# A new written-out order for the loop of a two-block vision kernel: fewer changes of TensorE's tiling

## Time and profile before

| | |
|---|---|
| runs of the kernel before | 370.17, 370.65, 375.33 us; median 370.65 |
| profiled execution, first to last instruction (its span) | 370.4 us |
| what lies around the span | 0.25 us, taken as the median less the span (the profile gives the profiled execution no other time than its span) |
| busy: PE, DVE, ACT, POOL | 331.5, 264.2, 235.4, 95.8 us |
| granted TensorE clock, mean of the span | 0.966 of 2.4 GHz |
| last matmul | starts 364.74, 1.08 us long |

### The profile page before, as it was taken

How to read it: one execution, slowest core, us unless ns; L and a number is a source line. 1 busy time by engine, 2 the same in 40 slices (tenths; PEclk the granted TensorE clock), 3 DMA queues, 4 the chain that set the end, 5 groups by cost and what they waited for, 6 DMA issues and landing times.

```text
span 370.4 us, 5249 instructions
## 1 busy us (share of the span) xinstructions
PE 331.5 (90%) x1709; PEld 177.8 (48%) x1709; DVE 264.2 (71%) x532; ACT 235.4 (64%) x448; POOL 95.8 (26%) x83
## 2 busy tenths in 40 slices
PE   8967999999967676789999899999999899898994
PEld 6556787878943133443434344344344344243230
DVE  3466978789543447779778969969958959947862
ACT  3533767778635453567678659769759766656653
POOL 6224374664410112412005103103105103102000
PEclk9989999999988969699999999999999999999999
DMA  5961000000000000039192193193193095075573
GB/s 152 146 202 32 3 1 2 0 3 2 2 0 2 0 1 0 0 112 354 43 386 86 33 357 117 33 356 115 35 374 96 4 327 173 0 259 215 191 308 65
DMA packets 27724, 42.48 MB, mean 115 GB/s; under 512 B 15857, under 2 KB 17649, under 8 KB 27697
## 3 DMA queue, kind: packets, MB, share of 16 engines
q1 hardware_dynamic: 27696, 42.14, 36.1%
HBM read 39.25 MB, written 2.88 MB: 114 GB/s over the span
## 4 chain that ended last, share of the span: by engine, by line
PE 32%; DVE 27%; DMA 12%; issue 10%; POOL 7%; SPq 6%; ACT 4%; POOLq 1%; ACTq 0%; DVEq 0%
DMA GB<-spread 9%; POOL rstdA L545 5%; PE ps L800 5%; PE ps L911 4%; PE ps L722 4%; DVE HB L1311 3%; PE ps L678 3%; DVE varA L1202 2%; SPq L486 2%; DVE XC L1311 2%; PE ps L709 2%; PE ps L690 2%; DMA spread<-GT 1%; DVE XN L1207 1%; DVE XN L1209 1%
## 5 line engine op out<-in xcount | busy, mean ns | idle before, releaser
L800 PE MATMUL ps<-ET,W1B 64*128 64x512 f32 x256 | 69.0, 641 | 1.4 <-ACT HB L1521 1.4
L1311 DVE TENSOR_TENSOR HB<-HB,GB 128x1024 f32<-128x1024 f32 x44 | 53.1, 1221 | 17.6 <-DMA GB<-spread 13.7
L1521 ACT ACTIVATE HB<-ps,B1B 128x1024 f32<-128x1024 f32 x44 | 48.1, 1114 | 15.5 <-PE ps L800 15.1
L545 POOL TENSOR_TENSOR rstdA<-varA,pow_half 128x8 f32<-128x8 f32 x16 | 30.4, 1897 | 74.1 <-DVE varA L1202 74.1
L911 PE MATMUL ps<-HB,W2B 128*64 128x512 f32 x176 | 44.8, 608 | 0.9 <-DVE HB L1311 0.9
L545 POOL TENSOR_TENSOR rstdB<-varB,pow_half 128x8 f32<-128x8 f32 x8 | 14.9, 1865 | 112.4 <-DVE varB L1244 112.4
L800 PEld LDWEIGHTS ps<-ET,W1B 64*128 64x128 f32 x256 | 21.3, 189 | 29.0 <-issue 17.7
L545 POOL TENSOR_TENSOR rstd<-var,pow_half 128x4 f32<-128x4 f32 (+1 forms) x24 | 29.1, 1219 | 22.9 <-DVE var L1015 13.9
L1311 DVE TENSOR_TENSOR XC<-XC,GB 128x1024 f32<-128x1024 f32 x20 | 24.1, 1220 | 7.1 <-DMA GB<-spread 6.7
L849 PE MATMUL ps<-VP,WC 128*128 128x512 f32 x96 | 27.3, 428 | 0.7 <-ACT VP L1484 0.7
L560 POOL TENSOR_TENSOR QS<-QS,rqsum 128x512 f32<-128x512 f32 x16 | 17.0, 1060 | 30.2 <-DVE rqsum L1076 30.2
(11 more groups left out here) (225 smaller groups left out, 627.7 us busy)
## 6 DMA issues: line engine op xcount, KB each, us to landing
GB<-spread SPq DMA_DIRECT2D x64, 512.0 KB, 8.0
out<-W1stage SPq DMA_DIRECT2D x8, 256.0 KB, 2.9
XC<-in_x SPq DMA_DIRECT2D x6, 256.0 KB, 5.7
G3R<-spread_r SPq DMA_DIRECT2D x48, 16.0 KB
T<-in_x SPq DMA_DIRECT2D x1, 512.0 KB, 3.7
W1A<-in_w1a SPq DMA_DIRECT2D x1, 512.0 KB
W1B<-in_w1b SPq DMA_DIRECT2D x1, 512.0 KB
spread_r<-KV SPq DMA_DIRECT2D x8, 64.0 KB, 9.9
```

The lines of the kernel that those rows point to most:

```text
L545: pool.tensor_tensor(out_, var, pow_half[:, 0:n], ALU.pow).then_inc(s[rstd_sem], 1)
L800: mm(ps[:, H_BANKS[n % 2][c], :], weights[half(c), :], tokens(half(c)), start=True, stop=True).then_inc(s["h"], 1)
L1311: tt(HG[b][e], HG[b][e], GB[:, e, :], ALU.mult).then_inc(s["f_hg"], 1)
L1521: av(HG[b][e], HID[n % 2], ACT.Gelu, bias=B1B[:, e:e + 1]).then_inc(s["gelu"], 1)
```

## The change

`FIRST`, `PLAN`, `LAST` and the code that expands them go; one list `LOOP` holds the whole order of the loop for each engine, every part with its image. The same parts stand in it, each once, with the same code, waits and buffers. The attention's order is also written out (`ATTENTION`), and is the same order; a part that issued nothing (`set_warm2`, zero matmuls; `order_rows` for pairs above 0) is dropped. The order on POOL is unchanged, and SP's code is not touched. On PE, ACT and DVE the order of the loop differs:

- **PE**: 137 runs instead of 154. Counted by stretches that end with `b_gates_turned:b` for b = 0 to 7, and the rest: before 11, 15, 18, 21, 21, 21, 23, 12, 12; after 11, 14, 18, 21, 17, 20, 17, 8, 11. The runs that go are 5 H, 7 O and 5 F.
- **PE, start**: `f_start:0` behind `b_gates:0`; `a_vT1:1` ahead of `f_hidden0:0 f_hidden1:0`; `b_conv0:1 b_conv1:1` ahead of `f_hidden2:0`.
- **PE, middle**: `b_conv0` and `b_conv1` side by side, and behind them `f_hidden4` beside `a_hidden1`; for image 2 and 3, `f_output5`, `f_hidden2` and `a_hidden0` of the next image stand ahead of or behind `b_gates_turned` in new places; `b_gates_turned:4` comes directly behind `f_hidden1:4`.
- **ACT and DVE** follow: at the start `a_square0:0` ahead of `a_select:1`, `a_z_copy:1` ahead of `a_select:2`, `b_exp:0` ahead of `a_image0:1 a_image1:1`, `f_gelu0:0` behind `b_gates_out:0`; in the middle `b_scale` ahead of `f_gelu4`; at the end several `f_gated:5` behind `a_normalise:7`.

The core of the diff, cut to TensorE's list and to the code:

```diff
-    for b in STEADY:
-        period(b, b % 2, PLAN[name], parts, image_exists)
-    in_order(LAST[name])
+    assert {token.split(":")[0] for token in LOOP[name]} == set(parts)
+    in_order(LOOP[name], parts)
...
     pe, start, before:
-        "a_z_turned:2 f_start:0 b_to_channels:0 b_gates:0 a_vT0:1 f_hidden0:0 f_hidden1:0 a_vT1:1 b_gates_turned:0 f_hidden2:0 "
-        "b_conv0:1 b_conv1:1 b_to_tokens:1 f_hidden3:0 f_hidden4:0 f_hidden5:0 f_output0:0 f_hidden6:0 f_hidden7:0 "
     and after:
+        "a_z_turned:2 b_to_channels:0 b_gates:0 f_start:0 a_vT0:1 a_vT1:1 f_hidden0:0 f_hidden1:0 b_gates_turned:0 "
+        "b_conv0:1 b_conv1:1 f_hidden2:0 b_to_tokens:1 f_hidden3:0 f_hidden4:0 f_hidden5:0 f_output0:0 f_hidden6:0 f_hidden7:0 "
...
     pe, the period before (b+1 is written +1):
-        "f_start f_output2-1 f_hidden0 f_hidden1 f_output3-1 f_output4-1 f_output5-1 b_gates_turned f_hidden2 "
-        "a_hidden0+2 a_vT0+1 f_hidden3 a_vT1+1 f_output6-1 b_conv0+1 f_hidden4 b_conv1+1 a_hidden1+2 b_to_tokens+1 "
-        "f_bias-1 a_output+2 f_output7-1 a_z_turned+2 f_hidden5 f_hidden6 f_output0 f_output1 b_to_channels+1 "
-        "f_hidden7 b_gates+1"
     and images 3 to 4 of the list after:
+        "f_hidden0:3 f_hidden1:3 f_output2:2 f_output3:2 f_output4:2 f_output5:2 f_hidden2:3 a_hidden0:5 "
+        "b_gates_turned:3 a_vT0:4 f_hidden3:3 a_vT1:4 f_output6:2 b_conv0:4 b_conv1:4 f_hidden4:3 a_hidden1:5 "
+        "b_to_tokens:4 a_output:5 f_hidden5:3 a_z_turned:5 f_bias:2 f_output7:2 f_output0:3 f_output1:3 f_hidden6:3 "
+        "b_to_channels:4 f_hidden7:3 b_gates:4 f_start:4 f_output2:3 f_output3:3 f_output4:3 f_hidden0:4 f_hidden1:4 b_gates_turned:4 "
...
     pe, the end of the list after, from a_output:7 on:
+        "a_output:7 f_hidden5:5 a_z_turned:7 f_bias:4 f_output7:4 f_output0:5 f_output1:5 f_hidden6:5 b_to_channels:6 b_gates:6 f_output2:5 "
+        "f_hidden7:5 f_hidden0:6 f_hidden1:6 f_hidden2:6 a_vT0:7 b_gates_turned:6 a_vT1:7 b_conv0:7 b_conv1:7 "
+        "b_to_tokens:7 f_output3:5 f_output4:5 f_output5:5 f_bias:5 f_start:6 f_output6:5 f_output7:5 f_output0:6 "
+        "b_to_channels:7 b_gates:7 f_hidden3:6 f_hidden4:6 f_start:7 f_output1:6 f_output2:6 b_gates_turned:7 "
+        "f_hidden5:6 f_hidden6:6 f_hidden7:6 f_hidden0:7 f_output3:6 f_hidden1:7 f_hidden2:7 f_output4:6 f_output5:6 "
+        "f_bias:6 f_hidden3:7 f_hidden4:7 f_output6:6 f_output7:6 f_output0:7 f_output1:7 f_hidden5:7 f_hidden6:7 "
+        "f_hidden7:7 f_output2:7 f_output3:7 f_output4:7 f_output5:7 f_output6:7 f_bias:7 f_output7:7"
```

More of the change, by code:

```diff
@@ L109 @@
     ).split(),
     act=(
-        "f_gelu5-1 a_select+2 b_channels f_gelu6-1 f_gelu7-1 b_exp a_square1+1 f_gelu0 f_gelu1 b_gates_out f_gelu2 "
-        "a_image0+1 a_image1+1 a_hidden0+2 f_gelu3 f_gelu4 b_scale+1 a_hidden1+2 a_z_copy+2 b_square+1 f_result-1 "
-        "a_square0+2"
[14 rows of a table added]
     ).split(),
 )
-ATTENTION_PLAN = dict(
+LOOP = dict(
     pool=(
-        "rstd2_3-1 rstd1_0+1 rstd1_1+1 qnorm2 rstd2_0 qnorm3 rstd2_1 qnorm0+1 qnorm1+1 rstd2_2"
+        "a_rstd0:0 a_rstd1:0 a_rstd0:1 b_rstd:0 a_rstd1:1 a_rstd0:2 a_rstd1:2 b_rstd:1 b_rstd:2 a_rstd0:3 a_rstd1:3 "
+        "b_rstd:3 a_rstd0:4 a_rstd1:4 b_rstd:4 a_rstd0:5 a_rstd1:5 b_rstd:5 a_rstd0:6 a_rstd1:6 b_rstd:6 a_rstd0:7 "
+        "a_rstd1:7 b_rstd:7"
@@ L120 @@
     ).split(),
     pe=(
[L122 to L146, removed]
[8 rows of a table removed]
[27 rows of a table added]
     ).split(),
@@ L157, with in_order @@
         "a_sum:0 a_ss0:0 a_zn:0 a_residual:0 a_centre:0 a_ss1:0 a_normalise:0 a_sum:1 a_ss0:1 a_zn:1 a_residual:1 "
[2 rows of a table removed]
[2 rows of a table added]
         "b_centre:1 f_gated0:0 b_ss:1 f_gated1:0 f_gated2:0 b_normalise:1 a_normalise:2 f_gated3:0 f_gated4:0 "
[3 rows of a table removed]
[17 rows of a table added]
     ).split(),
     act=(
[6 rows of a table removed]
[18 rows of a table added]
     ).split(),
 )
-LAST = dict(
-    pool=(),
-    pe=(
[7 rows of a table removed]
-    ).split(),
-    vec=(
[5 rows of a table removed]
-    ).split(),
-    act=(
[4 rows of a table removed]
[L197 to L200, removed]
 B_TOP = 14
 LOWEST = -3.0e38
-def parts_of(plan):
-    for token in plan:
-        name = token.rstrip("0123456789").rstrip("+-") if "+" in token or "-" in token else token
-        yield name, int(token[len(name):] or 0)
-def period(b, par, plan, parts, live):
-    for name, ahead in parts_of(plan):
-        if live(name, b, ahead):
-            parts[name](b + ahead, (par + ahead) % 2)
-def periods(name, parts):
-    def image_exists(name, b, ahead):
-        return 0 <= b + ahead < B
-    def in_order(tokens):
-        for token in tokens:
-            part, b = token.split(":")
-            parts[part](int(b), int(b) % 2)
-    assert sorted(parts) == sorted(part for part, _ in parts_of(PLAN[name]))
-    in_order(FIRST[name])
-    for b in STEADY:
-        period(b, b % 2, PLAN[name], parts, image_exists)
-    in_order(LAST[name])
-def pair_periods(name, parts):
-    parts, plan = dict(parts), ATTENTION_PLAN[name]
-    assert sorted(parts) == sorted(name for name, _ in parts_of(plan))
-    for p in range(-MOST_AHEAD, PAIRS + MOST_AHEAD):
-        period(p, p % 2, plan, parts,
-               lambda name, p, ahead: p + ahead == 0 or 0 < p + ahead < PAIRS and not name.startswith("set_"))
+def in_order(tokens, parts):
+    for token in tokens:
+        part, b = token.split(":")
+        parts[part](int(b), int(b) % 2)
+def periods(name, parts):
+    assert {token.split(":")[0] for token in LOOP[name]} == set(parts)
+    in_order(LOOP[name], parts)
+def pair_periods(name, parts):
+    parts = dict(parts)
+    assert {token.split(":")[0] for token in ATTENTION[name]} == set(parts)
+    in_order(ATTENTION[name], parts)
 def largest(vec, steps, p, n, vals, rev, m, eq, rank, q, onehot):
@@ L588, in _ @@
             mm = pe.matmul
-            WARM = (6, 2, 0)
+            WARM = (6, 2)
             def constant_products(bank, count):
@@ L760, in set_second @@
                 mm(ps[0:E, Q_BANK[1], 0:C], B2TA[:, :], ic[0:C, C:P], start=True, stop=True).then_inc(s["set_w2"], 1)
-            pair_periods("pe", [("set_second", set_second), ("set_warm0", set_warm(0)), ("set_warm1", set_warm(1)), ("set_warm2", set_warm(2)), ("set_fold", set_fold), ("set_outputs", set_outputs)] + [(f"{name}{h}", part(h)) for h in range(2) for name, part in (
+            pair_periods("pe", [("set_second", set_second), ("set_warm0", set_warm(0)), ("set_warm1", set_warm(1)), ("set_fold", set_fold), ("set_outputs", set_outputs)] + [(f"{name}{h}", part(h)) for h in range(2) for name, part in (
                                     ("centre", centre), ("xn_to_channels", xn_to_channels),
@@ L999, in part @@
                 def part(p, par):
-                    if p > 0:
-                        return
                     vec.wait_ge(s["ld_x0"], 16)
```

21 lines of the change are left out of this document (16 added, 5 removed), and 124 rows, old and new, of tables (act, pe, pool, vec).

## The result

The changed kernel takes **383.75 us** (median of 4 runs, 382.13 to 383.95) against 372.10 for the kernel before on the same chip (4 runs, 370.17 to 375.33): ratio 1.032, 95% interval 1.028 to 1.036. The forecast was 368.7 with a range from 363.5 to 373: the change was forecast as a gain and is a loss, and the time lies outside the range. The profiled execution has a span of 380.3 us, 9.9 more than before.

The account below looks back on a forecast made before the run. From 164 us on TensorE's own list was taken as the bound; before that, it often waits for a DVE, POOL and ACT chain. Span 370.4 + 0.7 - 1.4 - 0.4 - 0.9 + 0.1 = 368.5, with 0.25 368.7; range 363.5 to 373.

Parts of the forecast that it names:

- Start, forecast +0.7: Start of the loop: `b_to_tokens:1` starts at 164.15 instead of 163.48 us, so the start costs 0.7 us.
- I take 0.25 early: Start: wait before `a_hidden0:2` shrinks to about 1.8 us, clock stays full, `b_gates:0` comes 0.25 us early at 150.95.
- If the clock rises at 157.8 as before: Start: assumes full clock returns at 157.8 us, putting `b_gates_turned:0` at 158.5 instead of 157.84.
- Rival 2: Start: a 0.8 us gap keeps half clock until the convolution is done, +3.95 us, 372.6 in all; chance 0.15.
- a start at half clock twice over: Start: case put outside the range 363.5 to 373, together with an end without idle time under 2 in 10.
- A change of tiling: TensorE's list: each run costs beyond its parts 0.20 us for H, 0.15 for O, 0.20 for F.
- Rival 3: TensorE's list: joined parts of O and F save nothing, 0 and not 2.05 us, giving 370.75; chance 0.08.
- The number of runs: TensorE's list: 17 runs go, eight before `a_output:7` ends (-1.4 us) and nine behind (-1.6 us).
- The waits at `b_gates_turned`: Middle: TensorE's waits there sum to 2.6 us instead of 3.5, -0.9; bounds -3.5 and 0.
- End, forecast +0.1: From 306.58 us to the last matmul: walk gives 59.9, less six roundings 59.3, against 59.2; bounds -1.6 and +1.5.
- Rival 1: Whole kernel: TensorE's list is all that counts, start hidden, no new waits in the end, 365.3 us; chance 0.27.
- The base: Whole kernel: the median time lies 0.25 us above the span, so span 368.5 becomes 368.7.

Follow-up runs that it names:

- joined_conv: Kernel before with `b_conv1` put beside `b_conv0` and `f_hidden4` beside `a_hidden1` for images 3 to 6, 8 runs fewer: 371.06 against 371.02 us, ratio 0.998.
- end_only: Kernel before with the new order only in the end of the loop, nine runs fewer: 376.36 against 372.21 us, ratio 1.011.
- best_a: New start with 21 constant products, old middle with only eight pairs of parts joined, old end: 368.07 us against 372.03 for the kernel before, ratio 0.990.

## Why the prediction was wrong

The forecast for the span was 368.5; it was 380.3. The 11.8 us between are 0.3 ahead of the loop, 5.1 in the start, 2.9 in the middle, 3.5 in the end.

- **Start, forecast +0.7, measured +5.84. The step that failed is "I take 0.25 early"**: that the idle time before `a_hidden0:2` shrinks to about 1.8 us and the clock then stays full. The 1.8 was a slip in the working: with `a_hidden0:1` 2.0 later and `a_hidden0:2` 0.6 later, as the prediction has them, the wait of 3.96 shrinks to 2.6. It measured 2.65, and 2.6 is no longer close to the 1.6 that had left the clock at full. The clock fell all the same, 3.2 us later than before and so under `b_conv0:0`. Relative to the loop's start `b_gates:0` came 2.88 later than forecast. From there `b_gates:0` to `f_hidden0:0` took 4.73, forecast 4.70, at half clock as the forecast had it. Then the second assumption failed, "If the clock rises at 157.8 as before": hidden pair to `b_gates_turned:0` 3.72 instead of 2.85, from there to `b_to_tokens:1` 7.04 instead of 5.65. 2.88 + 0.03 + 0.87 + 1.39 = 5.2, the whole miss. Shown: filled with constant products, the same order takes 45.2.
- **Rival 2 named the mechanism** (gap ahead of the hidden pair, half clock until the convolution is done, the pair at 3.79, which is what it took) but priced one stretch, at 3.95. Two came, and "a start at half clock twice over" was left outside the range. Against its own full-clock time of 45.2 the start lost 8.2; the old start loses 1.8 (47.53 against 45.71), or 0.7 to 0.9 where its first hidden pair is at full clock.
- **A change of tiling, 0.15 to 0.20 per run: right** (`joined_conv`: 0.16 to 0.19). Lone parts cost what they did: a hidden part 1.06 (227.91 to 228.97), an output part 1.00 (219.00 to 220.00). Rival 3, and with it the rule of the Trainium skill (TensorE: Matmul & The Clock Gate, Part 3, The mechanism), would, as the prediction reads it, give `joined_conv` only the 4 runs of H, 0.8; the trace shows 1.3 to 1.6, so joining full-array parts saved time here too.
- **The number of runs: wrong.** The prediction counts `b_gates_turned` as full array, but the trace gives it as 128*64, the outputs' own tiling (it stands so in the earlier trace rows). Counted that way the list goes from 150 to 137 runs, in the middle from 99 to 95 and not from 105 to 97. Four runs at 0.18 and `f_bias:4` are 1.1; TensorE's busy time fell by 0.69 (138.78 to 138.09). Forecast were 1.8. What the last 0.4 are I have not isolated.
- **The waits at `b_gates_turned`, forecast 3.5 to 2.6: wrong in size.** The places were right: none at b = 3, one at b = 4, but that one took 1.70 and not 0.85; and `b_to_channels` waited 0.25 and 0.85, which I had not walked. For b = 5, 0.25 was forecast and 0.15 came. Idle time in the middle went up by 0.90 instead of down by 0.9. But this moves from execution to execution: the old middle took 141.28 to 143.10 in eight, the new one 139.88 to 143.68 in six without half clock. Most of that spread goes with one operation on POOL (last section), which the prediction took as fixed. The forecast gain of 2.7 is not there between the two orders as a whole.
- **End, forecast +0.1.** From `a_output:7` to `a_vT0:7` it took 15.71 (forecast 15.0), to `b_gates_turned:7` 22.29 (20.6; 20.94 with the products), to the last matmul 24.87 (24.3). The walk gave 59.9, and the 0.6 that the prediction takes off for roundings was not there. 0.6 + 0.7 + 0.35 + 0.55 for order and 1.35 for the clock make the 3.5. Of the 0.7, 0.5 go with `a_rstd0:7` on POOL, ahead of `a_normalise:7`: 2.55 us in all six executions with the new end, 2.0 in all with the old. The waits were foreseen one by one (behind `b_to_channels`, ahead of `a_vT0:7`, the convolution, `b_to_tokens:7`); that the clock would fall behind so many in a row was not.
- **Rival 1** (TensorE's list is all that counts, 365.3) falls with `end_only`, where nine runs fewer cost 1.1%, and with the start, where the list was as long as before. For the middle it is not refuted: in `best_a` a list 1.6 us shorter made the middle 1.6 us shorter, in `joined_conv` waits took most of it back.
- **The base.** The prediction puts 0.25 us around the span. In every run that shows both, the time is the span and some 1.8 us (382.13 and 380.3; 370.51 and 368.7; 367.95 and 366.2). Of the 15.05 us between 368.7 and 383.75, 11.8 are the span, 1.55 this, and 1.6 that the profiled execution was the fastest of the four; the rest is rounding.

## What to carry to other kernels

When an order is changed where TensorE waits often, price the clock first: a fall costs by what runs under it, so ask which long matmuls will stand in the 3 to 17 us behind each wait (so long did the half clock last here), and carry two falls in the range if there were two before. Recompute every shrunken wait from the two times that bound it. Constant products in the waits take the clock out of the question; judge an order with them in, and leave them in. Fewer changes of tiling save some 0.18 us of list each, and the time follows only where no wait grows by as much.
